# The input products of an attention, from three full-precision products to nine single-pass products of split operands

## The reference

```python
def _L1_attn_ref(x, qkv_w, qkv_b, rpb, proj_w, proj_b):      # K, H, DIM = 7, 16, 128
    qkv = (x @ qkv_w.T + qkv_b).reshape(B, L, 3, H, D).transpose(2, 0, 3, 1, 4)
    q, k, v = qkv[0] * SCALE, qkv[1], qkv[2]
    ni = jnp.clip(pos - K // 2, 0, L - K)
    idx = ni[:, None] + jnp.arange(K)
    attn = jnp.einsum('bhld,bhlkd->bhlk', q, k[:, :, idx]) + bias[None]
    attn = jax.nn.softmax(attn, axis=-1)
    out = jnp.einsum('bhlk,bhlkd->bhld', attn, v[:, :, idx])
    return out.transpose(0, 2, 1, 3).reshape(B, L, C) @ proj_w.T + proj_b

def _L1_ffn_ref(x, router_w, W1, b1, W2, b2):                # 6 experts, 341 hidden units
    ...  # router on the mean of a sequence, two of eleven partitions weigh the experts
    h = gelu(jnp.einsum('bsd,edf->ebsf', x, W1) + b1[:, None, None, :])
    out_e = jnp.einsum('ebsf,efd->ebsd', h, W2) + b2[:, None, None, :]
    return jnp.einsum('be,ebsd->bsd', expert_weights, out_e)

h = h + _L1_attn_ref(_layernorm(h), ...)
h = h + _L1_ffn_ref(_layernorm(h), ...)
```

## Time and profile before

| | us |
|---|---|
| median of 3 runs | 810.23 (808.23 to 811.02) |
| the profiled execution, its own time | 807.86 |
| its span, first to last instruction | 805.9 |
| PE busy | 611.8 (76%) |
| DVE busy | 631.9 (78%) |
| ACT busy | 526.9 (65%) |
| POOL busy | 281.3 (35%) |
| last stage, about | 522 to 806 |

### The profile page before, as it was taken

The page is one execution under the profiler, slowest core; times in us unless marked ns, Lnnn a source line. Parts: engine busy times, 40 slices in busy tenths (PEclk is TensorE's granted clock), DMA queues, the critical chain, the costliest instruction groups (busy, mean ns, idle before and its releaser), DMA issues.

```text
span 805.9 us, 10953 instructions
## 1 busy us (share of the span) xinstructions
PE 611.8 (76%) x3136; PEld 472.2 (59%) x3137; DVE 631.9 (78%) x1278; ACT 526.9 (65%) x849; POOL 281.3 (35%) x313
## 2 busy tenths in 40 slices
PE   6997651926446271929778899987999999999997
PEld 3564551826446271827455689844666666666665
DVE  1687498999999999999688622168899989988953
ACT  1489999999898999894232434352676576575542
POOL 0465100000000000000148744424367667665642
PEclk9998876859686786859976899998999999999999
DMA  5372042355544444452521466320000000000000
GB/s 185 115 269 80 1 71 50 66 99 103 99 93 75 88 87 76 81 97 48 171 71 31 135 176 181 101 74 1 1 1 9 2 11 11 1 11 10 0 11 20
DMA packets 26386, 56.53 MB, mean 70 GB/s; under 512 B 4204, under 2 KB 15573, under 8 KB 25861
## 3 DMA queue, kind: packets, MB, share of 16 engines
q0 software_dynamic: 5728, 24.56, 16.2%
q1 hardware_dynamic: 19848, 30.80, 12.5%
q10 hardware_dynamic: 764, 0.62, 0.2%
HBM read 29.91 MB, written 10.17 MB: 50 GB/s over the span
## 4 chain that ended last, share of the span: by engine, by line
DVE 35%; PE 30%; issue 15%; ACT 11%; DMA 4%; POOL 3%; SPq 1%; DVEq 0%; ACTq 0%; POOLq 0%
DVE s_R L1317 5%; DVE s_R L1304 4%; PE psum L1862 4%; DVE s_R L1328 4%; PE psum L2154 3%; DVE s_R L1776 3%; PE psum L2079 2%; PE psum L2071 2%; DVE s_R L1309 2%; PE psum L2141 2%; PE psum L2187 2%; DVE s_R L1623 2%; DMA s_R<-x_sorted 2%; PE psum L2143 1%; PE psum L2142 1%
## 5 line engine op out<-in xcount | busy, mean ns | idle before, releaser
L1934 PE MATMUL psum<-s_xn_lo,s_split_hi 128*128 128x368 f32 x256 | 94.3, 368 | 137.6 <-ACT s_R L945 134.8
L1934 PEld LDWEIGHTS psum<-s_xn_lo,s_split_hi 128*128 128x128 f32 x256 | 54.6, 213 | 142.2 <-ACT s_R L945 137.5
L702 POOL DMA_DIRECT2D s_xnfm<-s_R x14 | 17.1, 1219 | 256.1 <-DVE s_R L1328 256.1
L1323 DVE TENSOR_TENSOR_SCAN s_R<-s_R 128x2944 f32<-128x2944 f32 x16 | 100.7, 6291 | 0.8
L1935 PE MATMUL psum<-s_xn_hi,s_split_lo 128*128 128x368 f32 x256 | 91.3, 357 | 0.0
L1936 PE MATMUL psum<-s_xn_hi,s_split_hi 128*128 128x368 f32 x256 | 91.3, 357 | 0.0
L1089 ACT ACTIVATE s_xnfm<-psum,s_cols 128x368 f32<-128x368 f32 x96 | 49.4, 564 | 54.0 <-PE psum L2143 53.9
L2154 PE MATMUL psum<-s_xnfm,s_R 128*128 128x368 f32 x192 | 66.1, 479 | 0.7 <-DVE s_R L1646 0.7
L952 ACT ACTIVATE s_R<-psum,s_cols 128x736 f32<-128x736 f32 x64 | 55.9, 876 | 12.8 <-PE psum L1936 8.8
L762 POOL TENSOR_TENSOR s_R<-s_R 128x368 f32<-128x368 f32 x47 | 45.8, 974 | 38.3 <-DVE s_R L1646 18.3
L1304 DVE SCALAR_TENSOR_TENSOR s_R<-s_R 128x2944 f32<-128x2944 f32 x16 | 51.4, 3213 | 9.8 <-ACT s_R L910 6.4
(11 more groups left out here) (266 smaller groups left out, 1625.6 us busy)
## 6 DMA issues: line engine op xcount, KB each, us to landing
s_xnfm<-s_R POOLq DMA_DIRECT2D x14, 1472.0 KB, 10.5
s_R<-in_w SPq DMA_DIRECT2D x28, 256.0 KB, 2.9
s_R<-in_xg SPq DMA_DIRECT2D x7, 744.0 KB, 4.2
x_sorted<-in_x_init SPq DMA_DIRECT2D x1, 5082.0 KB
s_wBC<-in_wBC SPq DMA_DIRECT2D x8, 256.0 KB, 2.7
s_R<-in_v SPq DMA_DIRECT2D x2, 1024.0 KB
s_R<-x_sorted SPq DMA_DIRECT2D x28, 66.0 KB
s_R<-in_w SPq DMA_DIRECT2D x1, 1536.0 KB, 6.8
```

Of the source, the lines that this page charges most:

```text
L1323: dve.tensor_tensor_scan(bufB[:, u], ra[:, u], bufB[:, u], 0.0, ALU.mult, ALU.add).then_inc(ra_free, 1)
L1934: pe.matmul(bank(c), w_hi[:, s, u, k, :], xn_lo[:, a:b], start=True, stop=False)
```

## The change

The three input products of a chunk become nine: the weights of q, k and v are split once into `wq_hi` (ACT) and `wq_lo` (DVE) in the stage before, and the stream of each chunk is split into `xe_hi` (ACT, in place of the copy into `xfm`) and `xe_lo` (DVE, new, out of bank 7). The parts lie in unused columns of `xn_hi` and `xn_lo`. PE waits for `xe_split`, which DVE counts up, instead of for ACT's copy. In the loop two first-layer tiles, `ffn(f - 1, 14, 16)`, and their Gelus on ACT now go ahead of the input products and of their copies out.

```diff
@@ -455,6 +455,11 @@
+        xe_hi, xe_lo = xn_hi[:, TOK - CT:TOK], xn_lo[:, 4 * CT:5 * CT]
+        wq_hi, wq_lo = (xn_lo[:, 5 * CT + k * 3 * D:5 * CT + (k + 1) * 3 * D].rearrange("p (k d) -> p k d", k=3)
+                        for k in range(2))
+        wq_hi_ready, wq_split, xe_split = sem("wq_hi_ready"), sem("wq_split"), sem("xe_split")
@@ scalar @@
             load_table(ACT.Gelu, 0)
+            act.wait_ge(wE_ready, 6 * 16)
+            act.activation(wq_hi, w_qkv, ACT.Copy).then_inc(wq_hi_ready, 1)
...
+            def stream_hi(c, b):
+                act.wait_ge(nE.xT_ready, c + 3)
+                act.activation(xe_hi, bank(b), ACT.Copy).then_inc(nE.xT_free, 1)
...
             normed_e(0)
-            norm_copies(act, nE, 1, 0, (7, 7))
+            stream_hi(0, 7)
...
             normed_e(1)
-            norm_copies(act, nE, 0, 1, (7, 7))
+            stream_hi(1, 7)
             shares_out(0)
             qkv_out(1)
             for c in range(1, NCH + 2):
+                gelus(c - 2, 14, 16)
                 if 2 <= c < NCH:
                     qkv_out(c)
-                gelus(c - 2, 14, 16)
                 gelus(c - 2, 16, 18)
...
                 if c + 1 < NCH:
-                    norm_copies(act, nE, c % 2, c + 1, (7, 7))
+                    stream_hi(c + 1, 7)
                 gelus(c - 1, 12, 14)
@@ vector @@
             gate_scale()
+            dve.wait_ge(wq_hi_ready, 1)
+            dve.tensor_tensor(wq_lo, w_qkv, wq_hi.bitcast(f32), ALU.subtract).then_inc(wq_split, 1)
...
+            def stream_lo(c, b):
+                dve.wait_ge(nE.xT_free, c + 3)
+                dve.tensor_tensor(xe_lo, bank(b), xe_hi.bitcast(f32), ALU.subtract).then_inc(xe_split, 1)
...
             first_experts(0)
             first_experts(1)
+            stream_lo(0, 7)
             score_products(0)
...
             first_experts(2)
+            stream_lo(1, 7)
             shares_rest(0)
...
                 if 0 <= f - 1:
                     expert_weights(f - 1)
+                if 2 <= c < NCH:
+                    stream_lo(c, 7)
                 weigh_expert(f - 1, 0)
@@ tensor @@
             def qkv_of(c):
-                pe.wait_ge(nE.xT_free, c + 3)
+                pe.wait_ge(xe_split, c + 1)
+                if c == 0:
+                    pe.wait_ge(wq_split, 1)
                 if c > 1:
                     pe.wait_ge(pb_free, c * K)
                 for k, b in enumerate(qkv_banks(c)):
-                    pe.matmul(bank(b), w_qkv[:, k, :], fm(xfm, c), start=True, stop=True).then_inc(qkv_mm, 1)
+                    pe.matmul(bank(b), wq_hi[:, k, :], xe_lo, start=True, stop=False)
+                    pe.matmul(bank(b), wq_lo[:, k, :], xe_hi, start=False, stop=False)
+                    pe.matmul(bank(b), wq_hi[:, k, :], xe_hi, start=False, stop=True).then_inc(qkv_mm, 1)
...
             for c in range(1, NCH + 2):
+                ffn(f - 1, 14, 16)
                 if 2 <= c < NCH:
                     qkv_of(c)
-                ffn(f - 1, 14, 16)
                 ffn(f - 1, 16, 18)
```

More of the change, by code:

```diff
@@ L457, in audio_tower @@
         spread_r = xn_hi[0:OH, 4 * CT:4 * CT + K * D].rearrange("p (o d) -> p o d", o=K)
+        xe_hi, xe_lo = xn_hi[:, TOK - CT:TOK], xn_lo[:, 4 * CT:5 * CT]
+        wq_hi, wq_lo = (xn_lo[:, 5 * CT + k * 3 * D:5 * CT + (k + 1) * 3 * D].rearrange("p (k d) -> p k d", k=3)
+                        for k in range(2))
+        assert 4 * CT + K * D <= TOK - CT and 5 * CT + 6 * D <= TOK
+        wq_hi_ready, wq_split, xe_split = sem("wq_hi_ready"), sem("wq_split"), sem("xe_split")
         spread_ready, P_hi_ready = sem("spread_ready"), sem("P_hi_ready")
```

## The result

The changed kernel took 813.57 us (median of 11 runs, 810.87 to 816.07), the kernel before 809.58 us beside it (805.90 to 811.45): ratio 1.005, 95% interval 1.0033 to 1.0067, or +2.7 to +5.4 us. The profiled execution of the changed kernel took 812.41 us, its span is 810.6.

What follows compares the result with a forecast made beforehand. The prediction took DVE to set the pace at chunk boundaries, with a 1.05 us wait as its slack. Terms 0.45 + 1.44 + 0.6 + 0.8 - 0.1 gave +3.2 us on 810.23, so 813.4 us; range 810.5 to 816.

Steps and rivals of the forecast that it cites:

- signs named in advance: Trace observations in the start and loop, listed beforehand as showing the forecast right or wrong, such as the store's wait.
- a clock under 1.00 between 548 and 553 us: Start of the stage, PE: listed among the signs that would show the forecast wrong.
- Chunk 0: Start of the stage: PE's products wait for DVE's subtraction, so DVE's score products start later, +0.45 us.
- Chunk 1: Start of the stage: DVE's subtraction stands behind `first_experts(2)`, nine passes run alone, spreading starts late, +1.44 us.
- The clock: Rival, start: TensorE's clock falls in the new 1.8 us pause, nine passes take another 1.5 us, 814.9 us; chance 0.08.
- Chunk 2: Boundary without a result to store: DVE has no gap and waits for a later k, +0.6 us.
- Chunks 3 to 6: Loop boundaries: DVE's shift and collisions with POOL slightly exceed the store's wait, +0.2 us per chunk, +0.8 for four.
- Chunk 7: Last boundary: DVE already waits for k and has a gap, so the delay is absorbed, -0.1 us.
- Weights: Stage before: splitting the weights is covered by idle time of ACT and DVE, costing nothing; 0.5 us each without cover.
- PE-bound rival: Loop boundaries end with PE, so its saving and removed stall come back: 806.4 us, faster; chance 0.06.
- even boundaries: Rival: only the start and chunk 2 are paid, no collisions, +1.9 to +2.4 us, 812.1 to 812.6; chance 0.30.

Runs made afterwards that it cites:

- e3: Changed kernel with the f32 input products of before for chunks 0 and 1 alone: 811.03 us, ratio 1.0018 to the kernel before.
- e2: Changed kernel with two dummy products on PE in the pause ahead of chunk 1's input products: 813.52 us, ratio 1.0042 to the kernel before.
- e7: Changed kernel with POOL's bias add moved from the boundary to between its offset sums: 816.68 us, ratio 1.0082 to the kernel before.
- e1: Changed kernel with chunk 1's subtraction moved ahead of chunk 2's residual add and statistics on DVE: 811.89 us, ratio 1.0029 to the kernel before.
- e5: Changed kernel with the old order, nine passes and copies out ahead of the two first-layer tiles: 815.38 us, ratio 1.0072 to the kernel before.
- e6: Changed kernel with the loop's subtraction behind the two expert weighings on DVE: 812.93 us, ratio 1.0036 to the kernel before.
- e8: Changed kernel with the subtraction done twice on DVE for chunks 3 to 6: 815.16 us, ratio 1.0059 to the kernel before.
- e12: The changed kernel again, unaltered: 811.41 us, ratio 1.0050 to the kernel before (807.35 us on this chip).
- e11: Changed kernel with chunk 1's subtraction earlier, the loop's behind the expert weighings, and one first-layer tile ahead of the input products: 810.55 us, ratio 1.0041.
- e9: Changed kernel with f32 products for chunks 0 and 1 and the loop's subtraction behind the expert weighings: 807.43 us, ratio 0.9998 to the kernel before.

## Why the prediction was right, point by point

The forecast was +3.2 us, 813.4; measured +4.0 (+2.7 to +5.4), 813.57. That the two times agree to 0.2 us is luck: the kernel before ran at 809.58 beside it, not at the 810.23 that the forecast was added to, and this made up for the clock that the forecast had left out. Of the signs named in advance all those for it came, and one against it too: a clock under 1.00 between 548 and 553 us.

*Chunk 0*, +0.45: measured +0.34, and nothing in e3.

*Chunk 1*, +1.44: +1.45 with the clock held (e2; e7 gives 15.65 as well). The mechanism, a subtraction queued behind the add and statistics of chunk 2, is shown by e1, which takes half of it back by one moved line.

*The clock*, a rival at 0.08 with +1.5: it happened in five of the six profiles of this start (changed, e5, e6, e8, e12; leg A 16.99 to 18.08, that is +1.3 to +2.4), and not in e7, where it had been low from 536 to 546 and the pause was 1.33 us instead of 1.80. This is the step that the forecast had wrong: it put the clock at nothing, since the rows showed the fall only late in a pause of 3.98 us. In e5 and e12 the clock fell inside the pause of 1.80 us; in the changed kernel, e6 and e8 it fell 0.7 to 1.3 us into the nine passes behind it. That the pause brings the fall on is shown by e1 and e11, where it is 0.17 to 0.18 us, and e2, where it is filled: in these three profiles the fall doesn't come. The forecast and this rival came true together.

*Chunk 2*, +0.6: measured +0.67 (30.29 - 29.62). The reason was half right. k does come 0.44 us late (score products at 6.33 us behind the weights instead of 5.89; e9, which reaches them sooner, waits there for k until 6.34). But in the changed kernel they did not wait for it: DVE came as late by itself (1.08 us late at the add, which then took 0.68 us for 1.36), and the products took longer. DVE and POOL, before and after:

```profile
585.83 3.07 DVE L1686 TENSOR_TENSOR s_R<-s_R 128x344 f32<-128x344 f32 x7
```

```profile
585.71 3.24 POOL L768 TENSOR_SCALAR s_pa<-s_mv 92x4 f32<-92x4 f32 x1 [1.95 <-DVE s_mv L214]
```

```profile
589.76 4.00 DVE L1699 TENSOR_TENSOR s_R<-s_R 128x344 f32<-128x344 f32 x7
```

```profile
589.55 0.19 POOL L773 TENSOR_SCALAR s_pa<-s_mv 92x4 f32<-92x4 f32 x1 [2.34 <-DVE s_mv L214]
```

The products take 4.00 instead of 3.07. Before, POOL's first small operation began beside them and ended only when they did (588.95 for 588.90); now it takes 0.19 us, and POOL's further ones run beside the products. `weigh_rest` behind them got back 0.68 (0.89 for 1.57).

*Chunks 3 to 6*, +0.2 each: measured +0.20. The parts, against before: 1.10 us late at the add for 1.04, the add 1.21 for 1.25, the wait at the store wholly used, +0.07 behind the store for 0.1. e6 and e8 show what that rests on: half a microsecond earlier it is -0.2 against before, half a microsecond later still only +0.25. One reading of the prediction was wrong, though its sum is not touched. It took the add's 1.05 us before as undisturbed, but it was already held up, by another operation of POOL's. Alone it takes 0.68 (the same add at the start of the stage):

```profile
545.60 0.68 DVE L1587 TENSOR_TENSOR s_H<-s_R,s_H 92x512 f32<-92x512 f32 x1
```

```profile
642.41 0.97 POOL L762 TENSOR_TENSOR s_R<-s_R 128x368 f32<-128x368 f32 x1
```

This L762 ends at 643.38, and the DVE add of the earlier trace rows 0.55 behind it, at 643.93. So before, each of these chunks paid 0.37 us for a collision, and now pays 0.53.

*Chunk 7*, -0.1: -0.22. *Weights*, 0: nothing is seen of them in the ratios of e3 and e9, whose intervals leave room for 1 to 2 us; the legs start behind them and say nothing.

So the terms of order and work are 0.34 + 1.45 + 1.25 = 3.0 us, for a forecast of 3.2. The clock adds 1.3 us or more to leg A where it falls; the measured +4.0 has room for that, but what it costs in the time itself isn't resolved (e2). The PE-bound rival is out (the wait at the store went), and so is that of even boundaries (the add took 1.21 us).

## What to carry to other kernels

A faster product pays only up to the wait that it shortens: here PE saved 0.25 us per chunk and DVE had to pay for it with 0.46 us of splitting and 0.69 us of waiting. Place a new small operation where its input is already there, and look at who stands in order behind it on both engines; one line moved was worth 2.1 us in leg A. When two kernels differ by less than a per cent, compare fixed points of the trace leg by leg, since a leg of unchanged code varied by 2.9 us here.

## What the runs showed of the hardware

*Two adds on DVE and POOL that meet are not slowed a little; one waits for the other's end.* DVE's add at 648.28 met POOL's, which ended at 648.94, and ended 0.55 us behind that; a 4x6 operation took 0.88 instead of 0.22 us and ended with POOL's (e7); when DVE was 0.01 us ahead it lost nothing and POOL took 1.82 instead of 1.30 (e6). The Trainium skill (SBUF — State Buffer, SBUF: two separate sides) says that the port pair shared by the two is an exclusive lock that whichever starts first keeps for the whole instruction. It names the DVE instructions that this holds for: those with two SBUF inputs, against a GpSimd instruction that reads SBUF, and those in a two-port mode. The rows of the adds agree; the 4x6 operation reads a single tile, and no run here shows its mode. For an estimate it means that a shift of 0.5 us can cost 0.5 us or give it back.

*The clock comes back late and irregularly.* In leg B the low clock ended between 559 and 571 us, and the same code took 19.7 to 22.6 us. TensorE was busy for 6.98 of 9.00 us in e2's window, where it stayed low throughout. What decides when it returns wasn't tried.
